# Attention stage of an AdaLN block: weighted sums in pairs of chunks, the last 26 queries times four key quarters at once, score banks with own signals, plain output turns

## The reference, cut to what matters

```python
top_u = max(1, L // 5)                                   # 409 of 2048
_, top_idx = top_k(norm(Q, axis=2), top_u)               # per head, 64 heads (BH = 4 * 16)
Q_sel = take_along_axis(Q, top_idx)
scores = einsum('bud,bld->bul', Q_sel, K) / 32 ** 0.5
attn = softmax(scores, axis=-1)
out_sel = einsum('bul,bld->bud', attn, V)
out_full = zeros(BH, L, 32).at[:, top_idx].set(out_sel)
return out @ Wo.T + bo
```

## Time and profile before

| What | Value |
|---|---|
| Median of 3 runs | 3645.56 us (3643.36 to 3648.74) |
| Profiled execution, its own time | 3647.05 us |
| Its span | 3645.2 us |
| TensorE busy | 3308.7 us (91%) |
| VectorE busy | 2764.1 us (76%) |
| ScalarE busy | 1035.5 us (28%) |
| GpSimd busy | 1512.2 us (41%) |
| Mean granted TensorE clock | 0.957 |

### The profile page before, as it was taken

The page is one execution under the profiler, slowest core; times in us unless marked ns, Lnnn a source line. Parts: engine busy times, 40 slices in busy tenths (PEclk is TensorE's granted clock), DMA queues, the critical chain, the costliest instruction groups (busy, mean ns, idle before and its releaser), DMA issues. The chain is left out here.

```text
span 3645.2 us, 50953 instructions
## 1 busy us (share of the span) xinstructions
PE 3308.7 (91%) x16784; PEld 1498.4 (41%) x16784; DVE 2764.1 (76%) x3797; ACT 1035.5 (28%) x1454; POOL 1512.2 (41%) x1311
## 2 busy tenths in 40 slices
PE   5999997036999999999986999999999999999998
PEld 2554553021323332333323555555555555555554
DVE  4677675975666666666645898989898989898986
ACT  1332331003555555555541111111111111111111
POOL 0332331004555555555533444444444444445442
PEclk8999998567999999999997999999999999999999
DMA  5656556102222222222212100010101010101000
GB/s 185 180 181 208 177 176 196 44 1 66 68 73 72 72 73 68 73 67 74 72 41 81 32 30 32 29 32 29 32 29 32 29 32 29 32 29 32 29 23 15
DMA packets 194398, 252.71 MB, mean 69 GB/s; under 512 B 58581, under 2 KB 114261, under 8 KB 193493
## 3 DMA queue, kind: packets, MB, share of 16 engines
q1 hardware_dynamic: 177944, 245.07, 21.6%
q0 software_dynamic: 16384, 6.76, 1.2%
HBM read 154.68 MB, written 97.04 MB: 69 GB/s over the span
## 5 line engine op out<-in xcount | busy, mean ns | idle before, releaser
L1038 DVE TENSOR_REDUCE top<-ps_max 128x1 f32<-128x1024 f32 (+1 forms) x512 | 618.5, 1219 | 340.9 <-PE ps_max L1171 340.8
L1117 ACT ACTIVATE p<-ps_exp,p_bias 128x820 f32<-128x820 f32 x512 | 483.0, 943 | 457.6 <-PE ps_exp L1197 457.6
L1208 PE MATMUL ps_out<-p,v_tok 128*33 128x410 f32 x2048 | 453.0, 521 | 0.0
L1007 POOL DMA_INDIRECT o_d<-o_rows,chosen x256 | 249.0, 973 | 446.6 <-DVE o_rows L1064 373.7
L1642 ACT ACTIVATE silu<-f_g 128x512 f32<-128x512 f32 (+1 forms) x192 | 107.8, 561 | 801.5 <-PE f_u L1711 801.5
L1171 PE MATMUL ps_max<-k_max,q_max 96*128 96x512 f16 (+1 forms) x1024 | 314.4, 389 | 1.1 <-DVE top L1038 0.8
L1197 PE MATMUL ps_exp<-q_exp,k_exp 98*128 98x410 f16 x1024 | 266.7, 342 | 44.7 <-ACT p L1117 44.7
L1711 PE MATMUL f_g<-gu,xT_lo 128*128 128x512 f16 (+1 forms) x768 | 278.3, 362 | 0.0
L1709 PE MATMUL f_g<-gu,xT_hi 128*128 128x512 f16 (+1 forms) x768 | 278.1, 362 | 0.0
L1710 PE MATMUL f_g<-gu,xT_hi 128*128 128x512 f16 (+1 forms) x768 | 278.1, 362 | 0.0
L1709 PE MATMUL f_u<-gu,xT_hi 128*128 128x512 f16 (+1 forms) x768 | 277.5, 361 | 0.0
(11 more groups left out here) (201 smaller groups left out, 6417.7 us busy)
## 6 DMA issues: line engine op xcount, KB each, us to landing
k_max<-k_d SPq DMA_DIRECT2D x192, 128.0 KB
k_exp<-k_d SPq DMA_DIRECT2D x192, 128.0 KB
v_d<-v SPq DMA_DIRECT2D x16, 1056.0 KB, 7.5
v_tok<-v_d SPq DMA_DIRECT2D x64, 264.0 KB, 2.9
x<-in_x SPq DMA_DIRECT2D x16, 1024.0 KB, 6.5
q_d<-q SPq DMA_DIRECT2D x16, 1024.0 KB, 6.5
o_d<-zeros SPq DMA_DIRECT2D x16, 1024.0 KB, 8.5
a_in<-o_d SPq DMA_DIRECT2D x64, 256.0 KB, 2.6
```

Of the source, the lines that this page charges most:

```text
L1007: pool.indirect_dma_start(o_rows, bass.IndirectOffsetOnAxis(ap=con["chosen"][0:n, t, h:h + 1], axis=0), o_rows_of[u][0:n, t, :], None).the ...
L1038: ve.tensor_reduce(top[0:rows_of(t), t, half:half + 1], ps_max[c % 2][0:rows_of(t), :, :].rearrange("p a n -> p (a n)"), AX.X, ALU.max, ne ...
L1117: act.activation(p32[k % PB][:, :, :], ps_exp[:, :, 0:NQ], ACT.Exp, bias=con["p_bias"][:, 0:1], scale=scale).then_inc(p_done, 1)
L1208: last = pe.matmul(ps_out[at:at + VCOLS, 0:NQ], v_tok[u][:, t, :], p32[k % PB][:, s, :], start=k == 0, stop=k == STEPS - 1)
```

## The change

Four edits in `attend`, and one of names:

1. `weigh` is issued in pairs of chunks: steps 1, 3, 5 and 7 do two chunks each, in place of one chunk in every step. The constants of the order change: EARLY = 3, `turn_queries` in step 0, `turn_output` and `divide` in step 3, `rows` in step 6.
2. The maxima have CH = 7 chunks. The last tile of queries (26) is multiplied with the four quarters of the keys by four matmuls, which write partitions 0, 32, 64 and 96 of one bank. VectorE reduces 512 columns of it at once to `top_last`; the four maxima of a query now stand on four partitions, so `by_group` spreads them over 4 columns, the matmul `gather_last` brings them to 26 partitions by 4 columns in `ps_misc`, and `top_rows` takes their minimum from there. Step 4 has no chunk; `gather_last` stands in it.
3. The two banks of `ps_exp` get their own signals: every matmul of the scores counts `s_ready`, ScalarE has one instruction of 410 columns for each, and a matmul waits for its own bank alone.
4. `turn_output` is four plain transposes of `o32` (97 columns each); the sum of the two halves moves to `divide`, which now has a copy, a sum, a reciprocal and a product.
5. The semaphores that hold engines back at the start of a stage are shared between stages.

```diff
-    CH = 2 * QT
+    FULL = 2 * (QT - 1)
+    CH = FULL + 1
-    EARLY = 2
-    LAG = 3
-    QUERIES_AT = 3
-    OUT_AT = LAG
-    TURN_AT = 5
+    QUARTER = L // 4
+    EARLY = 3
+    QUERIES_AT = 0
+    OUT_AT = 1
+    TURN_AT = 3
+    GATHER_AT = 4
+    ROWS_AT = 6
...
         def chunk_of(k):
-            return (1, k + EARLY) if k + EARLY < CH else (2, k + EARLY - CH)
+            if k + EARLY < CH:
+                return (1, k + EARLY)
+            return (2, k - (STEPS - EARLY)) if k >= STEPS - EARLY else None
...
                     # VectorE, max_chunk
+                    if c < FULL:
+                        ve.tensor_reduce(top[:, t, half:half + 1], ps[:, :, :].rearrange("p a n -> p (a n)"), AX.X, ALU.max,
+                                         negate=True).then_inc(max_done, 1)
+                    else:
+                        ve.tensor_reduce(top_last[:, :], ps[:, 0, :], AX.X, ALU.max, negate=True).then_inc(max_done, 1)
+                        ve.wait_ge(max_done, h * CH + CH)
+                        need(ve, top_gathered, h)
+                        ve.tensor_scalar(by_group[:, :], group[:, :], top_last[:, 0:1], None, ALU.mult).then_inc(group_step, 1)
...
                     # VectorE, top_rows
+                    ve.tensor_reduce(top1[:, 0:QT - 1], top[:, :, :], AX.X, ALU.min).then_inc(top_step, 1)
+                    ve.wait_ge(top_gathered, h + 1)
+                    ve.tensor_reduce(top1[0:Q_LAST, QT - 1:QT], ps_misc[0:Q_LAST, 0:4], AX.X, ALU.min).then_inc(top_step, 1)
...
                     # VectorE, divide
+                    ve.tensor_copy(o_odd[:, :, :], turned[:, :, VTILE:OROWS]).then_inc(o_step, 1)
+                    ve.wait_ge(o_step, h * 3 + 1)
+                    ve.tensor_tensor(o_both[:, :, :], turned[:, :, 0:VCOLS], o_odd[:, :, :], ALU.add).then_inc(o_step, 1)
+                    ve.wait_ge(o_step, h * 3 + 2)
+                    ve.reciprocal(o_inv[:, :], o_both[:, :, HD]).then_inc(o_step, 1)
...
                 # VectorE, slot
                     for k in range(STEPS):
+                        if chunk_of(k) is not None:
+                            d, c = chunk_of(k)
+                            if has(i, d):
+                                max_chunk(i + d, (u + d) % 2, c)
                         if k == 0 and has(i, 1):
                             queries_again(i + 1, 1 - u)
                         if k == TURN_AT and has(i, -1):
                             divide(i - 1, 1 - u, stored_before(i, u, -1))
+                        if k == GATHER_AT and has(i, 1):
+                            top_rows(i + 1)
...
                 # ScalarE, exponentials
+                    for s in range(PER):
+                        act.wait_ge(s_ready, i * TILES + k * PER + s + 1)
+                        if s == 0:
+                            need(act, pv_done, i * STEPS + k - PB + 1)
+                        act.activation(p32[k % PB][:, s, :], ps_exp[s][:, 0:NQ], ACT.Exp, bias=con["p_bias"][:, 0:1],
+                                       scale=scale).then_inc(p_done, 1)
...
                 # ScalarE, slot
+                        exponentials(i, k)
+                        if k == QUERIES_AT + 1 and has(i, 2):
+                            take_queries(i + 2, u)
                         if k == OUT_AT and has(i, -1):
                             take_output(i - 1)
+                        if k == ROWS_AT and has(i, 1):
                             take_top(i + 1, 1 - u)
...
                     # TensorE, scores_for_max
+                    else:
+                        for j in range(4):
+                            last = pe.matmul(ps[j * HD:j * HD + Q_LAST, 0, :], q_max[u][:, t * P:NQ],
+                                             k_max[u][:, j * QUARTER:(j + 1) * QUARTER], start=True, stop=True)
...
+                def gather_last(h):
+                    pe.wait_ge(group_step, h + 1)
                     if isinstance(h, int) and h < 2:
                         pe.wait_ge(qsel_done, h + 2)
                     else:
                         pe.wait_ge(o_divided, h - 1)
+                    pe.matmul(ps_misc[0:HD, 0:4], same_row[:, :], by_group[:, :], start=True, stop=True).then_inc(top_gathered, 1)
...
                     # TensorE, scores
+                        n = k * PER + s
+                        need(pe, p_done, i * TILES + n - 1)
+                        pe.matmul(ps_exp[s][:, 0:NQ], k_exp[u][:, n * P:(n + 1) * P], q_exp[u][:, :], start=True, stop=True)\
+                          .then_inc(s_ready, 1)
...
                     # TensorE, turn_output
-                        last = pe.matmul(ps_misc[:, t * VCOLS:(t + 1) * VCOLS], o32[:, t * P:(t + 1) * P], fold[:, :],
-                                         start=True, stop=True)
+                        last = pe.transpose(ps_misc[:, t * OROWS:(t + 1) * OROWS], o32[:, t * P:(t + 1) * P],
+                                            con["ident"][0:OROWS, 0:OROWS])
...
                 # TensorE, slot
                     for k in range(STEPS):
                         scores(i, u, k, in_turn(i, u, 0))
+                        if k == TURN_AT and has(i, -1):
+                            turn_output(i - 1, i + 3 if has(i, 2) else None)
+                        if k == 1 and has(i, -1):
+                            for c in (STEPS - 2, STEPS - 1):
+                                weigh(i - 1, 1 - u, c, None)
+                        elif k % 2 == 1:
+                            for c in (k - 3, k - 2):
+                                if c >= 0:
+                                    weigh(i, u, c, in_turn(i, u, 0))
+                        if chunk_of(k) is not None:
+                            d, c = chunk_of(k)
+                            if has(i, d):
+                                scores_for_max(i + d, (u + d) % 2, c, in_turn(i, u, d))
                         if k == QUERIES_AT and has(i, 2):
                             turn_queries(i + 2, u)
+                        if k == GATHER_AT and has(i, 1):
+                            gather_last(i + 1)
+                        if k == ROWS_AT and has(i, 1):
                             rows(i + 1)
```

More of the change, by code:

```diff
@@ L240, in project @@
         f_ps = m.ps("f_ps", [P, N])
-        ve_held, pool_held, act_held, sp_held = (keep.sem(f"p1_{e}_held") for e in ("ve", "pool", "act", "sp"))
+        ve_held, pool_held, act_held, sp_held = (con["held"][e] for e in ("ve", "pool", "act", "sp"))
         bias_loaded = keep.sem("bias_loaded")
@@ L684, in choose @@
         pst = [m.ps(f"t_ps{k}", [P, 8, BH]) for k in range(2)]
-        ve_held = keep.sem("p2_ve_held")
+        ve_held = con["held"]["ve"]
         nrm_loaded, f_in = keep.sem("nrm_loaded"), keep.sem("f_in")
@@ L880, in attend @@
         q_exp = [m.sb(f"q_exp{u}", [KROWS + 2, NQ], F16) for u in range(2)]
-        top = m.sb("top", [P, QT, 2], F32)
+        top = m.sb("top", [P, QT - 1, 2], F32)
+        top_last = m.sb("top_last", [P, 1], F32)
+        by_group = m.sb("by_group", [P, 4], F32)
+        group = m.sb("group", [P, 4], F32)
+        same_row = m.sb("same_row", [P, HD], F32)
         top1 = m.sb("top1", [P, QT], F32)
@@ L889, in attend @@
         ps_max = [m.ps(f"ps_max{k}", [P, 2, 512]) for k in range(2)]
-        ps_exp = m.ps("ps_exp", [P, PER, 512])
+        ps_exp = [m.ps(f"ps_exp{s}", [P, 512]) for s in range(PER)]
         ps_out = m.ps("ps_out", [P, 512])
@@ L1181, in rows @@
                         pe.wait_ge(o_divided, h - 1)
+                    pe.matmul(ps_misc[0:HD, 0:4], same_row[:, :], by_group[:, :], start=True, stop=True).then_inc(top_gathered, 1)
+                def rows(h):
+                    pe.wait_ge(top_done, h + 1)
                     for t in range(QT):
@@ L1229, in first @@
                         scores_for_max(0, 0, c, 16)
+                    gather_last(0)
                     rows(0)
@@ L1301, in feed_forward @@
         ps_u = [m.ps(f"f_u{k}", [P, 512]) for k in range(2)]
-        ve_held, pool_held = (keep.sem(f"p4_{e}_held") for e in ("ve", "pool"))
+        ve_held, pool_held = (con["held"][e] for e in ("ve", "pool"))
         vec_in = {k: keep.sem(f"{k}_in") for k in ("ga", "sb", "cb", "gb")}
@@ L1793, in build @@
             "o_zeroed": keep.sem("o_zeroed"),
+            "held": {e: keep.sem(f"{e}_held") for e in ("ve", "pool", "act", "sp")},
         }
```

98 lines of the change are left out of this document (34 added, 64 removed).

## The result

The changed kernel took 3690.89 us (3685.93 to 3693.52, four runs) against 3645.56 (3643.36 to 3648.74, four runs) for the kernel before: 1.0122 times as long, 95% interval 1.0105 to 1.014. It is slower, by 45.3 us in the medians. The forecast was 3673 us within 3625 to 3708. The profiled execution took 3685.93 us with a span of 3684.1, 38.9 more than the span before.

The account below looks back on a forecast made before the run. Bound: TensorE's instruction stream plus its waits. Stream 13.67, ScalarE waits 0.63 and gather wait 2.0 gave 16.30 us a slot against 16.33; -3 us over the stage, +30 for the clock: 3673 us, range 3625 to 3708.

Parts of the forecast that it names:

- TensorE's stream: TensorE's own work in an attention slot: falls from 15.65 to 13.67 us, 2.66 less than the slot.
- Pair: Weighted sums two chunks at a time: eight changes of shape at 0.23 us become four, -0.92 us a slot.
- Last chunk: Last 26 queries: four column-tile matmuls stream together in 0.33 us instead of 1.08, -0.74 us a slot.
- Transposes: Output turn: four plain f32 transposes take 0.43 us instead of 1.01, -0.57 us a slot.
- The gather: New f32 matmul `gather_last` of 4 columns between two changes of tile shape: taken as +0.25 us a slot.
- The wait at the gather: Step 4, behind scores(4): TensorE stands still 2.0 us a slot for VectorE's late `divide`, bounds 1.6 and 2.4.
- The clock: Attention slots: the gather's wait brings half-clock stretches of 3.4 us in 20 of 62 slots, 1.5 us each, +30 us.
- Together some 0.63 us: TensorE's waits for ScalarE's exponentials before steps 3, 7 and 1: some 0.63 us a slot, bounds 0.3 and 1.0.
- That the clock holds: Rival: the gather's wait is there but the clock stays 1.00 in attention; 3643 us, 3622 to 3673; chance 0.30.
- The short wait: Rival: gather's wait 1 us or under from shorter VectorE steps, slot 15.3 us, about 3581 us; chance 0.10.
- That column tiles wouldn't overlap: Rival: the last queries' four matmuls run one after the other, +0.64 us a slot, 3683 us with clock held; chance 0.10.
- That the clock falls in nearly every slot: Rival: half-clock stretches in nearly all 62 attention slots, 93 us, 3736 us; chance 0.05.

Follow-up runs that it names:

- e1: Changed kernel with VectorE's `divide` of the previous head moved ahead of the last chunk's reduction, nothing else: 3591.91 us, ratio 0.985 to the kernel before.
- e2: Changed kernel with three more pairs of 512-column matmuls, result unused, ahead of the gather where TensorE waits: 3656.38 us, ratio 1.0031 to the kernel before.
- e3: Changed kernel with both banks of the scores under one signal again, one exponential of 820 columns: 3697.24 us, ratio 1.0138 to the kernel before.
- e4: Changed kernel with the output turn multiplied with `fold` again and `divide` back to two steps: 3646.19 us, ratio 1.0003 to the kernel before.

## Why the prediction was right, and the term that was mis-sized

**Sign, place and mechanism** held: TensorE stands still behind `scores(4)` 62 times for VectorE's product, it eats the savings, and the clock falls in part of the slots. e1 shows that the queue's order is the cause, e2 that the clock's part is a separate 30 us.

**TensorE's stream.** Pair 1.50 us as read (in and out 0.23 once for two chunks). Last chunk 0.33 for 0.33: four column tiles do stream together. The Trainium skill (TensorE: Matmul & The Clock Gate, the measured speedups of tiling), carried on from three tiles to four, gave an estimate of 0.08 more; the trace shows none of it. Transposes 0.43 for 0.43. The gather takes 0.14 from start to start where 0.25 was taken; its way in lies ahead of its start, in the 0.45 of the scores.

Two small readings in the stream were off. These are records of the kernel before, the second pair around its one wait:

```profile
1413.90 0.61 PE L1171 MATMUL ps_max<-k_max,q_max 96*128 96x512 f16 x2
1414.43 0.88 PE L1208 MATMUL ps_out<-p,v_tok 128*33 128x410 f32 x4
...
1415.61 0.60 PE L1171 MATMUL ps_max<-k_max,q_max 96*128 96x512 f16 x2
1416.89 0.52 PE L1197 MATMUL ps_exp<-q_exp,k_exp 98*128 98x410 f16 x2 [0.68 <-ACT p L1117]
```

The 0.68 counts from the end of a record, and here nothing lies over its last 0.17 us. From start to start TensorE stood still from 1415.61 + 0.43 to 1416.89, 0.85 us, so its stream was 16.33 - 0.85 = 15.48, where the sum took the busy time of 15.65. That is -0.17. Against it stand +0.10 that the sum lacks: in the changed order a plain chunk goes ahead of the matmuls of `rows`, and takes 0.53 (1417.89 to 1418.42) for 0.43, like the chunk ahead of weighted sums at 1413.90.

**The wait at the gather** was right. From the start of `scores(4)` to the gather the rows above give 0.12, 0.73, 0.14, 0.32, 0.33, 0.21 and 0.44, which is 2.29, and 2.39 in the slots of 16.62, whose product starts 0.10 later. The prediction's 2.46 begins 0.10 earlier, at the end of the last chunk's streaming, so 2.36 is to be compared. Less the 0.35 of the scores it is 1.94 or 2.04 us for 2.0; the 1.84 above takes off the gather's way in too. In the slot's sum the mean difference is -0.02.

**The clock**: 19 stretches of 3.4 us for 20 expected, 1.58 us each for 1.5, 30.0 for 30 us. The number of slots was an estimate between a quarter and a half, and that it came out near is luck more than reasoning: neither the one gap in two nor anything since says why 19, and e3, with the same wait, has 4. What the runs add: the clock held in the slots with waits of 0.68 (e1), 1.21 (e4) and, behind 1.46 us of matmuls, 0.56 (e2).

**The term that was mis-sized** is "Together some 0.63 us": the scores' waits for ScalarE. They are 1.10 us a slot, 0.47 more: 0.34 and 0.32 at step 3, 0.25 at step 1 and 0.19 at step 7; past the upper bound of 1.0. The step that failed is "A bank is free again 0.38 + 0.51 + 0.06 = 0.95 us after its scores start". Four exponentials of the changed kernel:

```profile
1409.13 2.14 ACT L1145 ACTIVATE p<-ps_exp,p_bias 128x410 f32<-128x410 f32 x4 [0.27 <-PE ps_exp L1236]
```

```profile
L1145 ACT ACTIVATE p<-ps_exp,p_bias 128x410 f32<-128x410 f32 x1024 | 557.7, 599 | 413.7 <-PE ps_exp L1236 406.2
```

One takes 0.60 us and the next starts 0.51 after it ((2.14 - 0.60) / 3). For ScalarE's load 0.51 was right; for the bank's release the whole 0.60 counts. And it starts 0.46 us after the scores (1408.67 to 1409.13), not 0.38: the prediction took one matmul's 0.17 off the 0.55 of before. So the bank is free after 1.12 us (1408.67 to 1409.79), 0.17 later than summed, and the second one, an exponential later, is late with it. Step 3 loses 0.66 us for 0.46, step 1 0.25 and step 7 0.19 for some 0.1 each.

**The sum**, then, a slot: 16.30 + 0.47 (ScalarE) - 0.17 and + 0.10 (stream) - 0.11 (gather) - 0.02 (wait) = 16.57; measured 16.53 and 16.62. Over 62 slots that is +15 us against the kernel before where -2 was forecast; with 30.0 for the clock, and about -6 in the remainder (-3.8 in the feed-forward stage, the rest at the ends), the 38.9 us of the two spans. The forecast of 3673 was 18 us low: 17 by the slots, where ScalarE's term alone is 62 x 0.47 = 29 and the others give back 12, and 6.5 since the profiled execution lay 5.0 us under the median where 1.5 above it was assumed; the remainder of -6 where -1 was summed takes off 5. So errors that cancel brought the forecast nearer than its worst term alone would have left it.

**The rivals.** That the clock holds: e2 is this case in the flesh, 3656 us where the rival had 3643 within 3622 to 3673, slower all the same, since the slot lengthened. The short wait needed shorter steps; e1 made it by an order instead, and gave 15.55 us a slot where the rival had 15.3. That column tiles wouldn't overlap is refuted. That the clock falls in nearly every slot didn't happen.

## What to carry to other kernels

When an edit takes work off the engine that bounds, ask which queue sets the next thing it waits for, and in what order that queue does things: here two calls exchanged on VectorE turned 1.2% slower into 1.5% faster, with the same instructions. A hand-over between engines is priced by the whole length of the instruction that releases and its start after the producer, not by the rate of such instructions back to back. Work that has no due time (here the maxima of later heads) is worth most where it covers such a hand-over: moving chunks, with VectorE's order to match, took the slot from 15.55 to 14.5 us.

## What the runs showed of the hardware

- An exponential of 128 x 410 from PSUM takes 0.60 us where a copy of 97 x 410 takes 0.50; in a row they start every 0.51. Two small ones (1.11 to the end of the second) are later than one of 820 columns (0.94), yet gained 0.5 us a slot by an earlier release.
- Four f16 matmuls of 512 columns (26 stationary) into output partitions 0, 32, 64 and 96 of one bank take 0.33 us together, way out included, where two plain ones take 0.43.
- Waits of TensorE of 1.8 us, once in a slot of 16.5 with TensorE busy for 14.4, can be followed by 3.4 us at the 1.2 GHz level; the stretches came at even distances, 51.2 us or 68.3. The same wait in slots of 17.1 us was followed by one 4 times in 62 only (e3). Not explained.
- On one of the chips, an engine that nothing in the trace held back started about a microsecond late, and the faster kernels lost more there than the kernel before (114 to 133 us against 20).
